# Token numbers listed as half-precision bit patterns, and both halves of the gate's weights in one product, in a graph-network, linear-attention and mixture-of-experts layer on one core

## The chip, the cores and the metric

The kernel runs on one core of one Trainium2 chip. The metric is the time of one execution on the device, in microseconds (us); lower is better. Durations of single instructions are in nanoseconds (ns) where marked so. The engines are named as the profile names them: PE (TensorE, matrix products), PEld (its weight loads), DVE (VectorE), ACT (ScalarE), POOL (GpSimd), SP (SyncE, which here only issues transfers).

## What is computed

6250 nodes with 512 features and 100000 edges, sorted by destination. With `xn` the normalised `x`:

```python
x = x + gnn(xn, src, dst) + mix(xn)           # graph part: mean over a node's in-edges, two products, norm;
                                              # mix: linear attention with 8 heads
x = x + ffn(layernorm(x))

def ffn(t):
    shared = gelu(t @ sw1.T + sb1) @ sw2.T + sb2          # 2 shared experts
    logits = t @ gate_w.T + gate_b                        # 8 routed experts
    probs = softmax(logits)
    top_v, top_i = top_k(probs, 2)
    routed = sum of top_v * expert[top_i](t)
    return shared + routed
```

The change touches two parts: `logits`, and the lists that say which tokens each of the 8 experts takes.

## The kernel before

Nodes are worked on in tiles of T = 125, two tiles (j = 0, 1) to a group, 25 groups in all (NG). Every operand of a precise product is held as a high and a low float16 half, and the helper `three` (lines 331 to 335) makes such a product of three matmuls: high by high, high by low, low by high.

The program has these stages: normalisation and keys with weight conversion (to about 396 us); **the group loop**, `group(i, prev, nxt)` on PE (line 1191), DVE (1863), ACT (872) and SP (451), beside `gathers` on POOL (line 615); a tail behind the last group, which ends the lists; the routed experts, which gather the listed tokens' rows (from line 1303 on PE, `rows_of` on POOL, line 658); and the shared experts with the sum (line 1360 on). Each engine has its own instruction stream, written out by hand; the order is fixed and semaphores alone tie the streams together.

In the group loop POOL gathers the source rows of a tile's edges with 17 indirect transfers to a tile (128 rows of 2 KB each), 9 of line 624 and 8 of line 631, 34 to a group. They go to two rings, one for j = 0 (shown as `Wff` in the profile) and one for j = 1 (shown as `region`). Before it refills a part of a ring POOL waits for PE to have used it (`agg_half`, `agg_ps`, lines 622 and 629). PE's `aggregate` (line 1135) multiplies the gathered rows with one-hot matrices (line 1151, 34 matmuls to a tile), and waits for the gathers of both parts (`gathered_a`, `gathered_b`). PE's order in `group(i, i-1, i+1)` is: the queries, the first mean turned, `aggregate(i, 1)`, the node's own product of tile 0, the second mean turned, `slot_list(prev-1, 0)`, the mean's product of tile 0, the denominators (line 1242), `turn_normalised(prev)`, the own product of tile 1, `slot_list(prev-1, 1)`, the mean's product of tile 1, `gate(prev)`, the spread denominators (line 1258), `aggregate(i+1, 0)`, `places(prev)`, the attention product.

**The gate.** PE's `gate` (line 1172) makes the logits of two tiles by `three` with 8 columns of weights `Wg`, 12 matmuls to a tile; DVE's `gate` (line 1798) scales them and adds the bias (line 1802), takes the maxima and their indices, and makes `chosen`, from which PE's `places` (line 1180) counts each token's place in its expert's list; DVE's `places` (line 1827) turns these counts into a column `posc` (which 128 places) and a row `posr` (which of them). DVE counts its steps on the semaphore `gate_dve`, 21 to a group (GATE_STEPS). In DVE's `group`, `gate(prev)` stands ahead of the scaled queries (lines 1918 and 1922), on which PE's attention product waits.

**The lists.** DVE's `listed` (line 1851) makes, for each of the two choices k of a tile's tokens, a one-hot of the column (`slot_c`, line 1859, 125 x 400 float16) and two matrices 125 x 128 that hold, at the token's row of places, the token's number within its tile (`own`, line 1860) and the first number of its tile (`tile_row`, line 1861). PE's `slot_list` (line 1123) adds four products of them into bank 7, 400 columns each (line 1127). After the last group DVE copies the bank into whole numbers (`idx_all`, line 1998), and SP (line 489) waits for that before it sends out the first list of indices (line 494), with which POOL's first gather of the routed experts begins (line 664).

In the trace `slot_p`, `slot_c`, `iota_c` and the first ring all lie in `Wff`, and `idx_all` in `ohs`.

The tail runs `gate(NG-1)`, `slot_list(NG-2, 0)`, `slot_list(NG-2, 1)`, `places(NG-1)`, the count, `slot_list(NG-1, 0)`, `slot_list(NG-1, 1)` on PE (lines 1290 to 1300), and on DVE lines 1954 to 1998.

## Time and profile before

| what | us |
|---|---|
| median of 3 runs | 2285.58 |
| lowest and highest of them | 2281.53, 2285.96 |
| the profiled execution, its time | 2284.43 |
| its span, first to last instruction | 2282.6 |
| PE busy, share of the span | 2074.4, 91% |
| DVE busy | 1567.9, 69% |
| ACT busy | 1089.6, 48% |
| POOL busy | 1323.6, 58% |

The span is what the hardware profiler recorded between the first and the last instruction; the execution's own time is 1.8 us longer, and the profiled execution lies 1.2 us under the median of the three runs. Busy time is the time in which an engine had an instruction at work; an instruction that issues a transfer to a ring on POOL counts, the wait for its data does not. The mean granted clock of TensorE was 0.972 of full speed.

### The profile page before, as it was taken

The numbers are of one execution on the slowest core, as the hardware profiler recorded it, in microseconds if no ns is written. First come the engines' busy times: TensorE is split into PE (matmuls) and PEld (weight loads), VectorE is DVE, ScalarE is ACT, GpSimd is POOL, SyncE is SP. The second block draws the span as 40 slices with busy tenths as digits, with TensorE's granted clock in tenths as the row PEclk, the third lists the DMA queues.
The fourth block names the chain that finished last, engine by engine and source line by source line (L and its number), as shares of the span: only waits on it lengthen the run. The fifth ranks groups of instructions, "written<-read, shape, count | busy, mean of one in ns | idle before, by whom it ended". The sixth has DMA issues, their size and how long they took to land. (4 is left out here: it accounts for less than half of the span.)

```text
span 2282.6 us, 46905 instructions
## 1 busy us (share of the span) xinstructions
PE 2074.4 (91%) x13232; PEld 1391.5 (61%) x13233; DVE 1567.9 (69%) x3840; ACT 1089.6 (48%) x2118; POOL 1323.6 (58%) x1370
## 2 busy tenths in 40 slices
PE   4997987899999999999999999993899999789998
PEld 2544554566666666666666666662666666557776
DVE  6887995567788777777787778775344444346666
ACT  3555674554655465546554655431344344323332
POOL 3665665777777777777777777740222222244443
PEclk9999999999999999999999999995999999989999
DMA  8647554788788788888888888873445455557675
GB/s 281 215 117 246 197 171 131 206 264 260 248 250 260 247 251 254 261 248 249 249 260 248 249 252 258 248 237 115 132 162 164 150 163 166 156 186 263 241 265 194
DMA packets 190000, 497.24 MB, mean 218 GB/s; under 512 B 42012, under 2 KB 54812, under 8 KB 188152
## 3 DMA queue, kind: packets, MB, share of 16 engines
q0 software_dynamic: 92720, 309.47, 45.6%
q1 hardware_dynamic: 66505, 135.52, 17.1%
q10 hardware_dynamic: 30719, 51.60, 6.0%
q8 instruction: 24, 0.39, 0.1%
q14 instruction: 32, 0.26, 0.0%
HBM read 373.91 MB, written 122.50 MB: 217 GB/s over the span
## 5 line engine op out<-in xcount | busy, mean ns | idle before, releaser
L664 POOL DMA_INDIRECT region<-table,idx x122 | 116.5, 955 | 359.3 <-PE bank L1315 268.9
L624 POOL DMA_INDIRECT Wff<-table,ebuf x225 | 235.7, 1047 | 69.0 <-issue 67.5
L624 POOL DMA_INDIRECT region<-table,ebuf x225 | 224.4, 998 | 84.0 <-issue 80.4
L333 PE MATMUL bank<-Wff,region 128*125 128x512 f16 (+1 forms) x636 | 245.1, 385 | 11.8 <-DVE region L2044 6.4
L631 POOL DMA_INDIRECT Wff<-table,ebuf x200 | 218.6, 1093 | 61.0 <-issue 61.0
L334 PE MATMUL bank<-Wff,region 128*125 128x512 f16 (+1 forms) x636 | 243.9, 384 | 0.0
L335 PE MATMUL bank<-Wff,region 128*125 128x512 f16 (+1 forms) x636 | 243.6, 383 | 0.0
L1151 PE MATMUL bank<-region,ohs 128*125 128x512 f16 x850 | 198.5, 389 | 45.0 <-DMA region<-table,ebuf 45.0
L631 POOL DMA_INDIRECT region<-table,ebuf x200 | 202.9, 1015 | 60.9 <-issue 60.9
L1151 PE MATMUL bank<-Wff 128*125 128x512 f16 x850 | 188.3, 380 | 0.0
L1151 PEld LDWEIGHTS bank<-region,ohs 128*125 128x125 f16 x850 | 114.5, 139 | 118.3 <-DMA region<-table,ebuf 55.6
L2009 DVE COPY region<-bank 128x1024 f16<-128x1024 f16 x60 | 41.5, 692 | 178.8 <-PE bank L1315 178.8
L333 PE MATMUL bank<-Wsn,region 128*125 128x512 f16 x400 | 152.9, 382 | 0.0
L1151 PEld LDWEIGHTS bank<-Wff 128*125 128x125 f16 x850 | 114.1, 137 | 63.5
L335 PE MATMUL bank<-Wsn,region 128*125 128x512 f16 x400 | 151.5, 379 | 0.0
L334 PE MATMUL bank<-Wsn,region 128*125 128x512 f16 x400 | 151.5, 379 | 0.0
L819 ACT ACTIVATE Wff<-iota_f,ebuf 128x125 f16<-128x125 f32 x425 | 125.9, 386 | 28.2 <-issue 28.2
L2016 DVE SCALAR_TENSOR_TENSOR region<-bank,sv,region 128x512 f32<-128x512 f32 x118 | 88.6, 750 | 71.4 <-PE bank L335 69.1
L819 ACT ACTIVATE ohs<-iota_f,ebuf 128x125 f16<-128x125 f32 x425 | 125.8, 386 | 17.9 <-DMA ebuf<-edges 14.2
L1326 PE MATMUL bank<-region,Wff 128*128 128x256 f16 x472 | 129.5, 274 | 1.9 <-DVE region L2009 1.9
L1327 PE MATMUL bank<-region,Wff 128*128 128x256 f16 x472 | 129.4, 274 | 0.0
L1328 PE MATMUL bank<-region,Wff 128*128 128x256 f16 x472 | 129.4, 274 | 0.0
(328 smaller groups left out, 5562.2 us busy)
## 6 DMA issues: line engine op xcount, KB each, us to landing
yd<-region ACTq DMA_DIRECT2D x59, 512.0 KB, 3.1
x2d<-region SPq DMA_DIRECT2D x25, 512.0 KB, 6.5
table<-region SPq DMA_DIRECT2D x25, 512.0 KB, 4.2
region<-x2d SPq DMA_DIRECT2D x25, 512.0 KB, 5.0
table<-region POOLq DMA_DIRECT2D x50, 250.0 KB, 3.4
xnt<-region POOLq DMA_DIRECT2D x25, 500.0 KB, 4.0
region<-xnt SPq DMA_DIRECT2D x25, 500.0 KB, 5.0
x2t<-region SPq DMA_DIRECT2D x25, 500.0 KB, 4.4
```

What stands on the lines that cost most here:

```text
L333: wmm(ps, xh, wh, start=first, stop=False)
L334: wmm(ps, xh, wl, start=False, stop=False)
L335: return wmm(ps, xl, wh, start=False, stop=last)
L624: pool.indirect_dma_start(out=ring[j][:, s, :], out_offset=None, in_=table, in_offset=bass.IndirectOffsetOnAxis(ap=ebuf[j][:, 2 * s:2 * s ...
L631: pool.indirect_dma_start(out=ring[j][:, s, :], out_offset=None, in_=table, in_offset=bass.IndirectOffsetOnAxis(ap=ebuf[j][:, 2 * s:2 * s ...
L664: pool.indirect_dma_start(out=tg[:, c, :], out_offset=None, in_=table2, in_offset=bass.IndirectOffsetOnAxis(ap=idx[:, 2 * turn + c:2 * tur ...
L819: act.activation(oh[j][:, s, :], iota_f[:], ACT.Abs, bias=ebuf[j][:, 2 * s + 1:2 * s + 2], scale=-1.0).then_inc(made_in, 1)
L1151: last = wmm(bank[6][0:T, :], oh[j][:, s, :], ring[j][:, s, part * D:(part + 1) * D], start=False, stop=False, skip_group_check=True)
L1326: wmm(ps, w1(e, 0, k, c), tTc[:, 0, k, :], start=(k == 0), stop=False)
L1327: wmm(ps, w1(e, 0, k, c), tTc[:, 1, k, :], start=False, stop=False)
L1328: last = wmm(ps, w1(e, 1, k, c), tTc[:, 0, k, :], start=False, stop=(k == KC - 1))
L2016: stt(ysb[:, j, :], bank[4 + j][:, :], sv[:, S_W2:S_W2 + 1], b2bc[:, e, :], ALU.mult, ALU.add).then_inc(sem["y_sb"], 1)
```

## The change

Two edits. **The lists:** a token's number plus 1024 is held as a 16-bit whole number, `id_bits`, and read as a float16 (`id_value`), so that one matrix `slot_p` for each choice takes the place of two. `slot_list` has two products in the place of four. The sum in bank 7 is copied to float16, its bits are read as whole numbers, and 1024 is taken away again (`idx_all`, now two instructions). `id_bits` is made in one DVE instruction ahead of the loop and raised by 256 in each group, and then copied to `id_value`; these take the place of `own`, of two memsets and of `tile_row`. **The gate:** the high half of a tile's rows is multiplied with both halves of the weights in one matmul of 16 columns, then its low half with the weights' high half in 8: 8 matmuls to a tile in the place of 12. The sum of the two halves' columns is made on DVE by a second `scalar_tensor_tensor`. GATE_STEPS goes from 21 to 23, and all waits on `gate_dve` go with it.

```diff
...
 I32 = mybir.dt.int32
+I16 = mybir.dt.int16
 U32 = mybir.dt.uint32
...
 HELD = 4
+ID_BASE = 1024
 OVER = NS + NE - HELD
...
         tok = sb("tok", [128, 2], I32)
-        own = sb("own", [128, 1], F32)
-        tile_row = sb("tile_row", [128, 2], F32)
+        id_bits = sb("id_bits", [128, 2], I16)
+        id_value = sb("id_value", [128, 2], F32)
         counted = sb("counted", [T, 1], F32)
...
         iota_c = over[0:T, spare:spare + COLS]
-        slot_p = over[0:T, spare + COLS:spare + COLS + 4 * 128].rearrange("p (k v n) -> p k v n", k=2, v=2)
+        slot_p = over[0:T, spare + COLS:spare + COLS + 2 * 128].rearrange("p (k n) -> p k n", k=2)
         behind = (OVER - 1) * FFB + 2 * TAIL
         slot_c = over[0:T, behind:behind + 2 * COLS].rearrange("p (k n) -> p k n", k=2)
-        assert spare + COLS + 4 * 128 <= (OVER - 1) * FFB and behind + 2 * COLS <= OVER * FFB - SLOTS // 2 * T
+        assert spare + COLS + 2 * 128 <= (OVER - 1) * FFB and behind + 2 * COLS <= OVER * FFB - SLOTS // 2 * T
         idx_all = ohs[:, 1200:1200 + 2 * COLS].bitcast(I32)
...
         den_rows = bank[2][0:TERMS, 128:128 + GT]
+        logits = bank[2][0:T, 0:4 * NE].rearrange("p (j v e) -> p j v e", j=G, v=2)
         half_ff = FFB // 2
...
             sp.wait_ge(sem["sched2_set"], 1)
-            sp.wait_ge(sem["idx_set"], 1)
+            sp.wait_ge(sem["idx_set"], 2)
             for e in range(NE):
...
             act.wait_ge(sem["yd_zero"], 16)
-            act.wait_ge(sem["disp_set"], 10)
+            act.wait_ge(sem["disp_set"], 8)
             onehots(0, 0)
...
             def gate(i):
-                act.wait_ge(sem["gate_dve"], GATE_STEPS * i + 6)
+                act.wait_ge(sem["gate_dve"], GATE_STEPS * i + 7)
                 if past(i):
-                    act.wait_ge(sem["gate_dve"], GATE_STEPS * (i - 1) + 11)
+                    act.wait_ge(sem["gate_dve"], GATE_STEPS * (i - 1) + 12)
                 for j in range(G):
...
             def slot_list(i, j):
-                pe.wait_ge(sem["slot_oh"], 12 * i + 6 * j + 6)
+                pe.wait_ge(sem["slot_oh"], 8 * i + 4 * j + 4)
                 for k in range(2):
-                    for v in range(2):
-                        last = wmm(bank[7][:, 0:COLS], slot_p[:, k, v, :], slot_c[:, k, :], start=False, stop=False, skip_group_check=True)
+                    last = wmm(bank[7][:, 0:COLS], slot_p[:, k, :], slot_c[:, k, :], start=False, stop=False, skip_group_check=True)
                 last.then_inc(sem["slot_ps"], 1)
...
                     for k in range(KC):
-                        last = three(bank[2][0:T, 8 * j:8 + 8 * j], tT[:, 0, k, both(j)], tT[:, 1, k, both(j)],
-                                     Wg[:, 0, k, :], Wg[:, 1, k, :], k == 0, k == KC - 1)
+                        wmm(logits[:, j], tT[:, 0, k, both(j)], Wg[:, :, k, :], start=(k == 0), stop=False)
+                        last = wmm(logits[:, j, 0, :], tT[:, 1, k, both(j)], Wg[:, 0, k, :], start=False, stop=(k == KC - 1))
                     last.then_inc(sem["gate_ps"], 1)
...
-                pe.wait_ge(sem["gate_dve"], GATE_STEPS * i + 9)
+                pe.wait_ge(sem["gate_dve"], GATE_STEPS * i + 10)
                 for j in range(G):
...
                 if older:
-                    pe.wait_ge(sem["gate_dve"], GATE_STEPS * (prev - 1) + 1)
+                    pe.wait_ge(sem["gate_dve"], GATE_STEPS * (prev - 1) + 2)
                 turn_mean(0)
...
                 if older:
-                    pe.wait_ge(sem["gate_dve"], GATE_STEPS * (prev - 1) + 12)
+                    pe.wait_ge(sem["gate_dve"], GATE_STEPS * (prev - 1) + 13)
                 turn_mean(1)
...
             turn_normalised(NG - 1)
-            pe.wait_ge(sem["gate_dve"], GATE_STEPS * (NG - 2) + 12)
+            pe.wait_ge(sem["gate_dve"], GATE_STEPS * (NG - 2) + 13)
             gate(NG - 1)
...
             dve.wait_ge(sem["sched_set"], 1)
-            dve.tensor_copy(own[:], tok[:, 0:1]).then_inc(sem["disp_set"], 1)
+            ts(id_bits[:], tok[:], float(ID_BASE - G * 128), None, ALU.add).then_inc(sem["disp_set"], 1)
             dve.memset(counted[:], 0.0).then_inc(sem["disp_set"], 1)
-            dve.memset(tile_row[:, 0:1], -G * 128.0).then_inc(sem["disp_set"], 1)
-            dve.memset(tile_row[:, 1:2], 128.0 - G * 128).then_inc(sem["disp_set"], 1)
             dve.wait_ge(sem["ident_set"], 10)
             dve.tensor_copy(iota_c, iota_n[0:T, :]).then_inc(sem["disp_set"], 1)
-            dve.wait_ge(sem["disp_set"], 10)
+            dve.wait_ge(sem["disp_set"], 8)
             halved(0, 0)
...
-                done, base = sem["gate_dve"], GATE_STEPS * i
+                done, base = sem["gate_dve"], GATE_STEPS * i + 1
                 dve.wait_ge(sem["gate_ps"], 2 * i + 2)
-                stt(gl[:], bank[2][0:T, 0:16].rearrange("p (j e) -> p j e", j=G), sv[0:T, S_G:S_G + 1],
+                stt(gl[:], logits[:, :, 0, :], sv[0:T, S_G:S_G + 1],
                     gateb_bc[0:T, None, :].broadcast_to([T, G, NE]), ALU.mult, ALU.add).then_inc(done, 1)
+                low_in = of(dve, base)
+                dve.wait_ge(sem["consts"], 1)
+                dve.wait_ge(done, low_in)
+                stt(gl[:], logits[:, :, 1, :], sv[0:T, S_G:S_G + 1], gl[:], ALU.mult, ALU.add).then_inc(done, 1)
                 logits_in = of(dve, base + 1)
...
-                done, base = sem["gate_dve"], GATE_STEPS * i
+                done, base = sem["gate_dve"], GATE_STEPS * i + 1
                 dve.wait_ge(sem["pos_ps"], i + 1)
...
                 stt(posr[:], posc[:], -128.0, posf[:], ALU.mult, ALU.add).then_inc(done, 1)
+                ts(id_bits[:], id_bits[:], G * 128.0, None, ALU.add).then_inc(done, 1)
+                dve.wait_ge(done, base + 21)
                 if past(i):
-                    dve.wait_ge(sem["slot_oh"], 12 * i)
-                ts(tile_row[:], tile_row[:], G * 128.0, None, ALU.add).then_inc(done, 1)
-                assert GATE_STEPS == 21
+                    dve.wait_ge(sem["slot_oh"], 8 * i)
+                dve.tensor_copy(id_value[:], id_bits[:].bitcast(F16)).then_inc(done, 1)
+                assert GATE_STEPS == 23
...
-                placed_in = of(dve, GATE_STEPS * i + 21)
+                placed_in = of(dve, GATE_STEPS * (i + 1))
                 dve.wait_ge(sem["consts"], 1)
...
                     ts(slot_c[:, k, :], iota_c, posc[:, j, k:k + 1], None, ALU.is_equal).then_inc(sem["slot_oh"], 1)
-                    ts(slot_p[:, k, 0, :], iota_c[:, 0:128], posr[:, j, k:k + 1], own[0:T, :], ALU.is_equal, ALU.mult).then_inc(sem["slot_oh"], 1)
-                    ts(slot_p[:, k, 1, :], iota_c[:, 0:128], posr[:, j, k:k + 1], tile_row[0:T, j:j + 1], ALU.is_equal, ALU.mult).then_inc(sem["slot_oh"], 1)
+                    ts(slot_p[:, k, :], iota_c[:, 0:128], posr[:, j, k:k + 1], id_value[0:T, j:j + 1], ALU.is_equal, ALU.mult).then_inc(sem["slot_oh"], 1)
...
             dve.wait_ge(sem["slot_ps"], 2 * NG)
-            dve.tensor_copy(idx_all, bank[7][:, 0:COLS]).then_inc(sem["idx_set"], 1)
+            listed_ids = gelc.rearrange("p c n -> p (c n)")[:, 0:COLS // 2].bitcast(F16)
+            dve.tensor_copy(listed_ids, bank[7][:, 0:COLS]).then_inc(sem["idx_set"], 1)
+            dve.wait_ge(sem["idx_set"], 1)
+            ts(idx_all, listed_ids.bitcast(I16), -float(ID_BASE), 0.0, ALU.add, ALU.max).then_inc(sem["idx_set"], 1)
...
-GATE_STEPS = 21
+GATE_STEPS = 23
 NORM_STEPS = 6 + 3 * NEWTON
...
```

## Rows read from the trace of the kernel before

**Rows 1.** Busy time by stretch; columns: stretch, length, engines' busy us, granted clock, DMA share.
```profile
396.00:1513.00 1117.00, 1071.19 (x6420) 725.39 (x6419) 856.15 (x2673) 616.00 (x1397) 863.41 (x833) 0.99 0.81 250
1513.00:1585.00 72.00, 42.38 (x234) 26.84 (x232) 48.63 (x191) 16.27 (x33) 4.42 (x9) 0.74 0.47 172
```

**Rows 2.** Groups of POOL, 395.6 to 1513.1 us; count, busy us, mean ns, idle before.
```profile
L624 POOL DMA_INDIRECT Wff<-table,ebuf x216 | 225.5, 1044 | 65.8 <-issue 64.3 <-DMA ebuf<-edges 1.5
L624 POOL DMA_INDIRECT region<-table,ebuf x225 | 224.4, 998 | 84.0 <-issue 80.4 <-DMA ebuf<-edges 3.4 <-PE bank L1151 0.3
L631 POOL DMA_INDIRECT Wff<-table,ebuf x192 | 211.0, 1099 | 58.5 <-issue 58.5
L631 POOL DMA_INDIRECT region<-table,ebuf x200 | 202.9, 1015 | 60.9 <-issue 60.9
```

**Rows 3.** Waits of 560 to 1570 us; us in total, times, longest.
```profile
PE bank L1151 <- DMA region<-table,ebuf: 30.7, 20, 2.5
```

**Rows 4.** Timeline of PE; start us, length us, instruction, count, idle before.
```profile
1021.12 0.84 PE L1127 MATMUL bank<-Wff 125*128 125x400 f16 x4
1021.80 0.38 PE L333 MATMUL bank<-Wsn,region 128*125 128x512 f16 x1
...
1518.38 3.67 PE L1151 MATMUL bank<-region,ohs 128*125 128x512 f16 x16 [2.47 <-DMA region<-table,ebuf]
...
1536.90 0.17 PE L333 MATMUL bank<-Wg,region 128*125 128x8 f16 x1
...
1538.20 0.20 PE L335 MATMUL bank<-Wg,region 128*125 128x8 f16 x1
...
1562.17 0.24 PE L333 MATMUL bank<-Wg,region 128*125 128x8 f16 x1 [1.25 <-ACT region L862]
...
1564.62 0.25 PE L335 MATMUL bank<-Wg,region 128*125 128x8 f16 x1
...
1568.96 1.52 PE L1127 MATMUL bank<-Wff 125*128 125x400 f16 x4 [2.74 <-DVE Wff L1861]
1570.27 0.21 PE L1185 MATMUL bank<-chosen,tri 125*125 125x8 f16 x1
```

**Rows 5.** Timeline of DVE: the instructions that the edits touch.
```profile
988.06 0.23 DVE L1802 SCALAR_TENSOR_TENSOR gl<-bank,sv,gateb_bc 125x16 f32<-125x16 f32 x1 [0.59 <-PE bank L335]
988.39 0.24 DVE L1808 MAX8 g<-gl 125x8 f32<-125x8 f32 x2
...
1567.45 0.33 DVE L1859 TENSOR_SCALAR Wff<-Wff,posc 125x400 f16<-125x400 f16 x1
...
1568.14 0.32 DVE L1859 TENSOR_SCALAR Wff<-Wff,posc 125x400 f16<-125x400 f16 x1
...
1583.47 0.56 DVE L1998 CAST ohs<-bank 128x400 int32<-128x400 f32 x1
```

**Rows 6.** Timeline of POOL in one group, gathers; the first of these is not held.
```profile
991.73 0.95 POOL L624 DMA_INDIRECT region<-table,ebuf  x1 [0.30 <-issue]
...
1013.62 1.42 POOL L624 DMA_INDIRECT Wff<-table,ebuf  x1 [0.30 <-issue]
...
1023.48 1.93 POOL L631 DMA_INDIRECT Wff<-table,ebuf  x1 [0.30 <-issue]
```

**Rows 7.** Timeline of DVE in that group: two-input instructions, and one of `listed`.
```profile
992.49 1.45 DVE L1922 TENSOR_TENSOR region<-region 128x500 f16<-128x500 f32 x2
...
1013.54 0.68 DVE L1876 TENSOR_TENSOR region<-region 128x500 f32<-128x500 f32 x1
...
1023.37 1.22 DVE L1886 TENSOR_TENSOR region<-region,beta_bc 125x1024 f32<-125x1024 f32 x1
...
1025.66 0.30 DVE L1861 TENSOR_SCALAR Wff<-Wff,posr,tile_row 125x128 f16<-125x128 f16 x1
```

**Rows 8.** Gather behind the last of these rows, on POOL.
```profile
1025.71 0.95 POOL L631 DMA_INDIRECT Wff<-table,ebuf  x1 [0.30 <-issue]
```

**Rows 9.** The stretch behind PE's wait at 466.5 us; columns as in the first group.
```profile
466.50:468.50 2.00, 2.00 (x5) 1.20 (x6) 0.00 (x0) 0.00 (x0) 1.39 (x3) 0.50 0.61 193
```

## The prediction

> **What bounds the kernel now.** I read the busy time by stretch first. The group loop, 396 to 1513 us, takes half of the time; in it PE is busy for 1071 of 1117 us at full clock, DVE for 856 and POOL for 863 [rows 1]. So PE looks like the bound, and the change takes work off PE. The rows of POOL say otherwise. Its 833 gathers take 863.8 us together, and 269 us of idle time stand before them, of which only 0.3 us was ended by PE [rows 2]. The idle time is 0.30 us before each gather [rows 6], some 250 of the 269 us, and for the rest one gap near the start of the loop: after it POOL issues gather behind gather, and never waits for a free ring. A group takes 45.7 us, 34 gathers at a pitch of 0.95 + 0.30 us (42.7 us), and 3.0 us more because some take longer than 0.95 us. PE for its part waits for gathered rows in 20 of 22 groups, 30.7 us in all [rows 3], and 2.47 us for the last gathers of all, at 1518.38 [rows 4]. **POOL's issue of gathers paces the loop**; PE has about 1.4 us to spare in each group (30.7 / 22). The tail, 1513 to 1585 us [rows 1], is a chain through DVE and PE with no such cover.
>
> **The products of the lists, on PE.** Four products of 400 columns take 1021.80 - 1021.12 = 0.68 us, 0.17 each [rows 4]. Two fewer in each of 50 tiles: 100 x 0.17 = 17 us of PE's time, 0.68 us in a group. At half clock in the tail four take 1570.27 - 1568.96 = 1.31 us [rows 4], so two fewer save 0.65.
>
> **The gate's products, on PE.** 24 small matmuls start 23 pitches apart in 1538.20 - 1536.90 = 1.30 us, 0.057 each; eight fewer save 0.46 us in a group, 11 us in 25. In the tail at half clock the pitch is (1564.62 - 1562.17) / 23 = 0.107, and eight fewer save 0.85 [rows 4]. That one product has 16 columns instead of 8 I price at nothing; if columns counted, 8 more at 2.4 GHz are 0.003 us each, 0.03 us for eight.
>
> **DVE.** One matrix fewer for each choice: two instructions of 0.23 us pitch (three starts in 1568.14 - 1567.45 = 0.69 us [rows 5]) in each tile, 0.46 us. The second instruction on the logits waits for the first; the next dependent step starts 988.39 - 988.06 = 0.33 us behind it [rows 5], so it costs 0.33. In `places` one more dependent step costs between nothing and 0.33; I take 0.2. The final list is now copied to float16 and then converted: the copy as before 0.56 us [rows 5], and behind it a step of 400 elements from SBUF that the trace does not show; between 0.3 (the 400-column step of `listed` in SBUF, 0.32 [rows 5]) and 0.65 us (a second pass like the first, with a wait), I take 0.45. Three tiny steps at the start go, next to nothing, beside POOL's gap.
>
> **In the loop** PE saves 0.68 + 0.46 = 1.14 us in each of some 24 groups, 27 us in all, and none of it reaches the end by itself: PE arrives 1.14 us earlier at rows that land when POOL has issued them, and its wait of about 1.4 us grows to 2.5, the last one from 2.47 to 3.6. What can reach POOL is one thing. A gather is held while DVE runs an instruction with two tensors from SBUF: the one of 1023.48 took 1.93 in place of 0.95 us and lies in line 1886's (1023.37 to 1024.59); the one of 1013.62 took 1.42 and lies in line 1876's (1013.54 to 1014.22) [rows 6, 7]. Both fit one rule: 0.13 us after its start a gather waits for the end of such an instruction (1024.59 - 1023.61 = 0.98; 1014.22 - 1013.75 = 0.47). Eight holds of that kind stand in the group: 0.07, 0.26, 0.20, 0.47, 0.43, 0.17, 0.98 and 0.15 us, at the lines 1922, 1930, 1935, 1876, 1796, 1707, 1886 and 1907; over the 816 gathers they make the 3.0 us a group. The change adds and removes no such instruction (the new ones read one tensor from SBUF), but it moves some. DVE is 0.81 us earlier from line 1918 to 1941 (1.14 on PE, less 0.33), 0.6 earlier at 1876 and 1796, 0.45 earlier at 1907, and not moved at 1707 and 1886, which follow PE's wait. By the rule, in the same group: line 1922 then covers the gather of 991.73 (992.36 - 991.86 = 0.50 in place of 0.07), the next ones give 0.27 and 0.19, line 1876 0.50, line 1796 misses by 0.05, 0.12, 0.98 and none: 2.56 in place of 2.73 us. That is -0.17 a group, -4 us over 24. But two of these misses are by less than 0.1 us, and each group starts from where the one before left off; I take -0.1, **-2.5 us**. Its bounds: one hold of average size (0.4) more in every group is +9.6 us, one and a half fewer -14.
>
> **In the tail** every step counts, from PE's last wait on. Two pairs of list products, -0.68, and the gate -0.46; the second logit step +0.33: -0.81 at the attention product. The last gate at half clock -0.85, its second step +0.33: -1.33. Then `listed` -0.46, its products -0.65, `places` +0.2, `listed` -0.46, products -0.65, `listed` -0.46 (each waits for the other [rows 4, 5]): -3.81. The last conversion +0.45: **-3.4 us**, bounds -2.5 and -4.5. The routed and shared experts get the same lists: nothing.
>
> **The sum.** The profiled execution took 2284.43 us, 1.2 under the median of 2285.58: 2284.43 - 3.4 - 2.5 = 2278.5 there, and 2279.7 against the median.
>
> **A rule weighed against the trace.** Line 1861's instruction at 1025.66 to 1025.96 covers the point 1025.84 of the gather of 1025.71, and that gather took 0.95 us, not held [rows 7, 8]. So I price the removal of its like at nothing for POOL. The Trainium skill (SBUF - State Buffer, the rules on the shared port pair) has a VectorE instruction in a two-port mode, which a float16 one with a single tensor can be, lock GpSimd out as well; by that the sum would have a further gain, the fifth case below. The same page has two tensors from SBUF contend with a GpSimd instruction that reads SBUF, and there the trace agrees, 0.98 us of it at line 1886.
>
> **The rivals.**
> 1. *The holds fall much lighter.* Six moved instructions cost about 1.6 us a group; if in every group one hold of the size of line 1876's stays out, it is -0.5 a group, -12: 2285.6 - 3.4 - 12 = 2270. For it: one hold (line 1796, 0.43) goes by 0.05 us already. Against: the new one at line 1922.
> 2. *The holds fall heavier: slower.* If the gathers met the moved instructions at random, each of length L would cost L x L / (2 x 1.25), 1.25 us being the pitch of the gathers; the six kinds come to 1.97 us a group against 1.6 now, +0.35, +8.4: 2285.6 - 3.4 + 8.4 = 2290.6. It decides as soon as the holds grow by more than 0.14 us a group, where they eat the tail's gain. For it: the present places are lighter than chance.
> 3. *PE's clock falls in the longer wait.* Behind a wait of PE for gathers early in the loop, the one that ends at 466.5 us, the granted clock was 0.50, half of 2.4 GHz, for at least 2 us [rows 9]. Half clock for 4 us costs PE 2 us, which its spare 2.5 us cover in the loop. Behind the last gathers nothing covers it: +2 in the tail, 2281.7. Against: over the whole loop the granted clock was 0.99 [rows 1], waits and all.
> 4. *PE paces the loop after all* and its 27 us come through: 2285.6 - 3.4 - 27 = 2255.2. Against: 0.3 us of POOL's waits are PE's [rows 2].
> 5. *The removed instructions did hold gathers.* 92 of 0.31 us in the loop, by the formula above 0.04 each, 3.5 us more: 2279.7 - 3.5 = 2276. Against: the gather of [rows 8]. The page for it is the one of the Trainium skill named above.
>
> **How the numbers follow.** What a measurement of this kernel can tell from no change is about 0.2%, 4.6 us. My forecast, with 2276 to 2284 as its own range, has 0.42, of which 0.22 lies below 2281.0 and 0.20 above. Rival 1 has 0.19, all faster; rival 2 0.16, of which 0.13 slower; rival 3 0.15, 0.12 of it the same and 0.03 faster; rivals 4 and 5 0.04 each. Faster 0.22 + 0.19 + 0.03 + 0.08 = 0.52; the same 0.20 + 0.03 + 0.12 = 0.35; slower 0.13. The range leaves out rival 4, the light end of rival 1 and the heavy end of rival 2: 2267 to 2290.
>
> **What would show it.** PE busy in the loop falls by some 27 us and its waits for gathers grow by about 1.1 us in each group; POOL still shows no idle time that PE ended; POOL's gathers have a mean near 1034 ns (now 1037); the time from the end of PE's last wait to the first copy of the list falls from 65.1 us (1583.47 - 1518.38 [rows 4, 5]) by 3.9 to 61.2, and the conversion then takes 0.45 more. Wrong would be: a POOL that waits for `aggregate`, a change in the 0.95 us of an unheld gather, or a loop that is shorter by PE's 27 us. If the mean of a gather moved by more than 10 ns, the holds decided and not the work removed.

## The result, and the profile after

The changed kernel takes 2258.42 us (median of 4 runs, 2253.56 to 2261.71), the kernel before beside it 2285.30 (4 runs, 2281.53 to 2285.96): a ratio of 0.9889, 95% interval 0.9876 to 0.9902. It is 26.9 us faster. The forecast was 5.9 us faster, and its range ended at 2267. The profiled execution took 2260.08 us.

The head of its page, then busy time by stretch (columns as in [rows 1]):

```profile
span 2258.5 us, 46325 instructions
PE 2050.2 (91%) x12932; PEld 1370.3 (61%) x12933; DVE 1552.0 (69%) x3789; ACT 1089.0 (48%) x2118; POOL 1304.6 (58%) x1370
```

```profile
396.00:1490.00 1094.00, 1045.95 (x6095) 702.92 (x6094) 834.25 (x2608) 616.99 (x1400) 840.21 (x829) 0.99 0.82 255
1490.00:1560.00 70.00, 44.61 (x266) 29.80 (x263) 51.28 (x190) 16.27 (x33) 8.71 (x13) 0.79 0.49 171
```

POOL's groups in the loop, which answer to [rows 2], and PE's waits for gathers, which answer to [rows 3]:

```profile
L627 POOL DMA_INDIRECT region<-table,ebuf x225 | 225.0, 1000 | 85.2 <-issue 84.0 <-DMA ebuf<-edges 1.2
L627 POOL DMA_INDIRECT Wff<-table,ebuf x216 | 211.0, 977 | 65.8 <-issue 62.5 <-DMA ebuf<-edges 3.3
L634 POOL DMA_INDIRECT Wff<-table,ebuf x192 | 205.2, 1069 | 58.5 <-issue 58.5
L634 POOL DMA_INDIRECT region<-table,ebuf x200 | 203.5, 1017 | 61.0 <-issue 61.0
```

```profile
PE bank L1153 <- DMA region<-table,ebuf: 28.6, 17, 2.4
```

The idle time of POOL is what it was: 0.30 us before each gather, one gap near the start, nothing that PE ended. The gathers themselves are shorter. I count from the 35th gather, the first behind that gap, to the last, 816 in all. What a gather takes over 0.95 us I call its hold, and the instant 0.125 us behind its start its point. Before, the holds add up to 70.9 us, after to 51.6 us: **19.3 us less, a mean of 1013 ns for 1037**. The gaps between them add up to 248.4 us in both. The 24.1 us by which the span fell are, from the two traces: the 35th gather 1.8 later (418.60, 420.41), holds -19.3, last gather's end to the last aggregation product +1.2, that product to the first load of the list -3.8, and the part of the experts -4.0 (697.7 to 693.7 us), which this change does not touch. In that part PE's waits for the routed experts' rows (lines 1315 and 1317) go from 44.4 to 39.8 us with the same products: 4 of the 24.1 us are no work of the edit that I can name.

A sum of the holds by the line of VectorE whose end the held gather waited for, in us over the 24 groups (some 2 us of small ones fit no line), with what the prediction's followed group would give (its holds times 24):

```
step (line before/after)    before   after   moved   forecast
beta added (1886/1891)       22.5    19.3    -3.3      0
q + rest (1876/1881)          9.8     0.6    -9.2     +0.7
low half of table (1796)      9.3     2.6    -6.7    -10.3
halves (1707/1709)            7.6     6.8    -0.8     -1.2
low half of q (1922/1927)     6.3     6.0    -0.4    +10.3
hh steps (1930,1935/1935,1940) 10.5  10.7    +0.2      0
den terms (1907/1912)         2.9     0      -2.9     -3.6
lines 1714, 1865, 1916        0.1     3.8    +3.7      0
```

One group after the change, POOL's gathers, then VectorE beside them:

```profile
1011.69 0.95 POOL L627 DMA_INDIRECT Wff<-table,ebuf  x1 [0.30 <-issue]
...
1018.07 1.43 POOL L634 DMA_INDIRECT Wff<-table,ebuf  x1 [0.30 <-issue]
...
1021.06 1.94 POOL L634 DMA_INDIRECT Wff<-table,ebuf  x1 [0.30 <-issue]
```

```profile
1011.68 0.72 DVE L1881 TENSOR_TENSOR region<-region 128x500 f32<-128x500 f32 x1 [0.40 <-ACT region L890]
...
1017.99 0.68 DVE L1709 TENSOR_TENSOR Wff<-Wff 128x1000 f16<-128x1000 f16 x1 [1.59 <-issue]
...
1020.96 1.22 DVE L1891 TENSOR_TENSOR region<-region,beta_bc 125x1024 f32<-125x1024 f32 x1
```

Two of the three gathers obey the prediction's rule: the gather of 1018.07 reaches its point at 1018.20 and waits for 1018.67, that of 1021.06 waits for 1022.18. The first does not. Its point, 1011.82, lies inside line 1881's instruction (1011.68 to 1012.40), and the gather takes 0.95 us. It is the VectorE instruction that is longer, 0.72 in place of 0.68.

The tail, PE, VectorE and SP (these answer to the last rows of [rows 4, 5]):

```profile
1502.07 1.29 PE L1153 MATMUL bank<-region,ohs 128*125 128x512 f16 x5 [1.83 <-DMA region<-table,ebuf]
```

```profile
1562.94 0.56 DVE L2004 CAST region<-bank 128x400 f16<-128x400 f32 x1
1563.54 0.37 DVE L2006 TENSOR_SCALAR ohs<-region 128x400 int32<-128x400 int16 x1
```

```profile
1564.77 0.60 SPq L497 DMA_DIRECT2D idx<-ohs  x1
```

From the end of PE's last wait to the first copy of the list it is now 60.87 us; 65.1 before, 61.2 forecast.

### The profile page after: what moved, and what is told of

Its sections match the earlier page's. It is cut to its first block and busy times, and to the rows that moved or that the text cites. A ratio compares the mean times of both kernels' runs of the same rounds, so it can differ in the third digit from the quotient of the medians.

```text
span 2258.5 us, 46325 instructions
## 1 busy us (share of the span) xinstructions
PE 2050.2 (91%) x12932; PEld 1370.3 (61%) x12933; DVE 1552.0 (69%) x3789; ACT 1089.0 (48%) x2118; POOL 1304.6 (58%) x1370
## 5 line engine op out<-in xcount | busy, mean ns | idle before, releaser
L627 POOL DMA_INDIRECT Wff<-table,ebuf x225 | 221.1, 983 | 69.1 <-issue 65.7
L634 POOL DMA_INDIRECT Wff<-table,ebuf x200 | 212.8, 1064 | 61.0 <-issue 61.0
L1153 PE MATMUL bank<-region,ohs 128*125 128x512 f16 x850 | 205.1, 398 | 41.9 <-DMA region<-table,ebuf 41.9
L338 PE MATMUL bank<-Wff,region 128*125 128x512 f16 (+1 forms) x636 | 242.9, 382 | 0.0
L338 PE MATMUL bank<-Wsn,region 128*125 128x512 f16 x400 | 151.5, 379 | 0.0
```

The lines of the kernel that those rows point to most:

```text
L338: return wmm(ps, xl, wh, start=False, stop=last)
L627: pool.indirect_dma_start(out=ring[j][:, s, :], out_offset=None, in_=table, in_offset=bass.IndirectOffsetOnAxis(ap=ebuf[j][:, 2 * s:2 * s ...
L634: pool.indirect_dma_start(out=ring[j][:, s, :], out_offset=None, in_=table, in_offset=bass.IndirectOffsetOnAxis(ap=ebuf[j][:, 2 * s:2 * s ...
L1153: last = wmm(bank[6][0:T, :], oh[j][:, s, :], ring[j][:, s, part * D:(part + 1) * D], start=False, stop=False, skip_group_check=True)
```

## Experiments

### Ten runs in which POOL did not pace the loop: e1 to h1

The theory, as the first traces gave it: POOL's gathers pace the loop, and the holds decide. Its rival: PE's shorter work was what was gained (27 us removed, 26.9 us gained, a coincidence of numbers that needed a test). Edits of the first series: the lists' part alone (e1, f2), the gate's part alone (e2), the whole change with PE's time given back (e3, f1), and the whole change with the addition of beta made on one tensor (e4, h1), which leaves beta out of the result. The two edits that are not parts of the change:

```diff
...
+                if j:
+                    for _ in range(PAD):
+                        wmm(bank[6][0:T, :], zeros16[0:1, 0:T], zeros16[0:1, :], start=False, stop=False, skip_group_check=True)
                 with pe.Fori(lo, hi) as r:
...
+PAD = 5
...
-                tt(xg, xg, beta_bc[0:T, None, :].broadcast_to([T, G, D]), ALU.add).then_inc(sem["h_gam"], 1)
+                ts(xg, xg, 1.0, None, ALU.mult).then_inc(sem["h_gam"], 1)
...
```

e1: 

> The changed kernel with the gate of before: 24 small matmuls, one DVE instruction on the logits. Theory H (holds): POOL paces the loop, so the time follows the sum of what gathers take over 0.95 us, and not PE's work; that sum can lie anywhere between 50 and 75 us, and the time is 2285 less the tail's 2 us, less the fall of that sum from 70.9 us. Theory W (work): PE's removed time comes through, 0.68 us a group, 17 us: about 2266, with the sum of holds beside the point.

e2: 

> The kernel before with the change's gate alone. Theory W: 0.46 us a group of PE's work less, 11 us: 2274. Theory H: DVE's later instructions come only 0.13 us earlier (0.46 less 0.33), so the holds stay near 70.9 us and the time near 2284; whatever it is, time and holds move by the same amount within 3 us.

e3: 

> The changed kernel with 5 matmuls of 512 columns with zeros more in each group, directly ahead of PE's wait for the second tile's gathered rows: about 1.07 us a group, 27 us of PE's work, as much as the change took away. Theory W: the whole gain is lost, 2285. Theory H: PE's wait shrinks by about 1 us a group, POOL waits for nothing, and the time stays at 2258, within the few us that moved holds make.

e4: 

> The changed kernel with the sum of x and beta replaced by a product of x with 1.0, so beta is left out of the result; DVE then reads one tensor from SBUF in place of two, in an instruction that may run in a two-port mode. It held a gather in 24 groups of 24, for 19.3 us in all. Theory H with the two-tensor rule alone: these holds go, 19 us less, about 2240. If a one-tensor instruction in a two-port mode holds as well, as the 400-column step of the lists did for 0.1 us: it is about half as long, its holds are 0.3 us on the average and some 8 us stay: 2248. Theory W: no change in the loop, 2258.

Measured, ratios to the kernel before: e1 1.0231 (1.0159 to 1.0304), e2 0.9981 (0.9941 to 1.0022), e3 1.0212 (1.0155 to 1.0270), e4 1.0039 (1.0012 to 1.0066). But **the kernel before itself took 2962.7 us** there, not 2285, and on three other chips 2963.0 (f1, f2), 3001.6 (g1 to g3) and 3004.7 (h1). The repeats gave 1.0174 (f1, as e3) and 1.0258 (f2, as e1). Then the change itself and two kernels with PE's work in the loop cut (g2 the kernel before, g3 the changed one; the products of the low halves are left out), to let POOL pace:

g1: 

> The changed kernel itself once more. In the first experiments the kernel before took 2963 us in the place of 2285, because PE waited for its own instructions inside the loop. Theory H (holds): where POOL does not pace the loop neither holds nor their fall reach the end, so the gain of the loop, 19 us, is gone, and only the tail's 4 us are left; where the kernel before takes 2285 again, the change takes 2258. Theory W (work): fewer instructions on PE are fewer to wait for, 300 of some 6700 in the loop, so the change gains more here than before, 4% of the loop's 1790 us, some 70 us.

g2: 

> The kernel before with PE's work in the group loop cut: of the queries', own, mean and attention products only high by high, and of the gathered rows only the high half is added (the result is less exact). PE has some 120 instructions and 20 us fewer in each group. Theory H: POOL paces the loop again, the gap between gathers is 0.30 us, a group takes 42.7 us and the holds, and the loop ends near 1510 us whatever PE has to do.

g3: 

> The changed kernel with the same cut. Theory H: in both thin kernels POOL paces the loop; their difference from the first gather of the loop to the last is the difference of their sums of holds within 2 us, although the change takes the same 1.14 us of PE's work a group away. Theory W: the thin changed kernel's loop is shorter by 27 us, or by nothing if PE's work is covered, with no tie to the holds.

g1 has a ratio of 0.9942 (0.9920 to 0.9964), g2 0.9066, g3 0.9024. The trace of g1 says what was different. POOL's first two groups in its loop, the loop's stretch, and PE in it:

```profile
L627 POOL DMA_INDIRECT region<-table,ebuf x225 | 227.0, 1009 | 439.3 <-DMA ebuf<-edges 361.2 <-issue 78.1
L627 POOL DMA_INDIRECT Wff<-table,ebuf x216 | 219.9, 1018 | 454.0 <-DMA ebuf<-edges 395.2 <-issue 58.8
```

```profile
396.00:2217.00 1821.00, 1312.75 (x6006) 777.25 (x6004) 825.57 (x2568) 604.14 (x1371) 823.85 (x833) 0.76 0.52 153
```

```profile
1018.04 0.27 PE L1203 MATMUL bank<-region,Wq 128*128 128x250 f16 x1
1018.67 0.27 PE L1204 MATMUL bank<-region,Wq 128*128 128x250 f16 x1 [0.36 <-issue]
1020.85 0.27 PE L1205 MATMUL bank<-region,Wq 128*128 128x250 f16 x1 [1.92 <-issue]
1023.02 0.37 PE L1203 MATMUL bank<-region,Wq 128*128 128x250 f16 x1 [1.90 <-issue]
```

Up to 1018.04 one product starts each 0.11 us; then one each 2.17 us, behind idle time that "issue" ended, so that nothing in the profile held it. Such stretches fill the loop of groups, and the granted clock falls to 0.76 with them; the last group, whose instructions are written out behind the loop, has none (its 48 query products take 5.3 us, those of a group in the loop some 22). POOL waits for edge lists, some 940 to 1030 us of gaps between the 816 gathers in place of 248. So these runs can't test which of POOL and PE paces the loop of the kernel as it ran at 2285, and none of their ratios is read. The thin kernels did not mend it: gaps of 681 and 647 us. What the runs do give is the hold itself, which needs no pace: behind the addition of beta, 10.2 to 11.4 us in e1, e2, e3 and g1, and 2.0 us in e4, where that step has one tensor. h1 was to use both:

> The changed kernel once more with the addition of beta left out (the step has one tensor in place of two, so beta is not added). In the run of the changed kernel the gathers of the group loop stood 19.3 us behind that step. Theory (POOL's gathers pace the loop, and a DVE step with two tensors holds a gather): if the kernel before takes about 2285 us again, this kernel takes 14 to 19 us less than the changed kernel's 2258, so about 2241, a ratio of 0.981 to the kernel before, and the holds behind that line fall from 19.3 to under 3 us. Rival (the holds lie in time that the loop has anyway): 2256 to 2259, ratio 0.989, though the holds fall. If the kernel before takes about 2965 us, as in the runs so far, POOL does not pace the loop, both expect a ratio of 1.00 as in e4, and the run tells the theories apart by the holds alone.

It came out at 0.9988 (0.9965 to 1.0010) beside 3004.7, holds of that line 2.9 us, within the second case of its expectation, and tells no more than e4.

### The loop written out: i1 and i2

The same instructions in the same order on every engine, without the jump back. PE's loop, one of five that are written out alike:

```diff
...
-            with pe.Fori(2, NG - 1) as i:
+            for i in range(2, NG - 1):
                 group(i, i - 1, i + 1)
...
```

i1: 

> The kernel before with the loop over the groups written out on all five engines (the same instructions in the same order, but no jump back at a group's end). In the runs so far of this series the kernel before took 2963 to 3004 us because the instructions in the body of that loop start late (48 query products 20 us, 5.0 us in the last group, which is written out). If it is the loop that makes them late, this kernel takes about 2285 us, a ratio near 0.76 to 0.78, its gathers stand back to back again (idle between the 816 about 250 us) and POOL paces the groups. If the supply is late whatever the form, it takes 2960 to 3000 us, ratio 1.00.

i2: 

> The changed kernel with the loop over the groups written out in the same way. If POOL's gathers pace it, theory (holds behind two-tensor steps of VectorE decide): 2254 to 2264 us, 24 to 30 us under the unrolled kernel before, with the time of the 816 gathers over 0.95 us near 51 us against 71 us (change of the holds equal to the change of the time before the tail within 3 us). Rival (the work removed on TensorE decides, and the holds are along for it): 24 to 30 us less though the holds differ by under 10 us. If the supply stays late: within 0.6% of the unrolled kernel before.

On this chip the kernel before took 2281.06 us with its loop as it is, so whether writing out cures the late supply stays open. Nor does the chip alone decide it: g1 to g3 and k1 to k4 below ran on the same one, with 3001.6 and 2283.0 us for the kernel before. From here on every kernel ran as the first did, at 2281 to 2284 for the one before, and POOL paced the loop. i1 took 2269.79 us, ratio 0.9957 (0.9940 to 0.9973); i2 2268.34, ratio 0.9947 (0.9930 to 0.9963). POOL's groups in the loop of i1, then of i2:

```profile
L624 POOL DMA_INDIRECT region<-table,ebuf x225 | 222.7, 990 | 83.5 <-issue 80.4 <-PE bank L1151 2.7 <-DMA ebuf<-edges 0.3
L624 POOL DMA_INDIRECT Wff<-table,ebuf x216 | 219.0, 1014 | 65.8 <-issue 65.5 <-DMA ebuf<-edges 0.3
L631 POOL DMA_INDIRECT region<-table,ebuf x200 | 206.3, 1031 | 61.0 <-issue 60.6 <-PE bank L1151 0.3
L631 POOL DMA_INDIRECT Wff<-table,ebuf x192 | 202.1, 1053 | 58.5 <-issue 58.5
```

```profile
L627 POOL DMA_INDIRECT region<-table,ebuf x225 | 221.4, 984 | 83.2 <-issue 82.6 <-DMA ebuf<-edges 0.6
L627 POOL DMA_INDIRECT Wff<-table,ebuf x216 | 218.4, 1011 | 65.8 <-issue 64.9 <-DMA ebuf<-edges 0.9
L634 POOL DMA_INDIRECT region<-table,ebuf x200 | 206.1, 1031 | 61.0 <-issue 61.0
L634 POOL DMA_INDIRECT Wff<-table,ebuf x192 | 204.7, 1066 | 58.5 <-issue 58.5
```

The busy times add up to 850.1 and 850.6 us. The holds are 57.1 us in both, and the last gather ends at 1498.38 and 1498.60. The change takes the same products off PE here and is worth 1.5 us in the medians, with the tail 4.0 shorter. I had expected i2 to keep the whole gain and the gap between the holds (51 against 71); that missed, but what theory ties together stayed together: no fall of the holds, no gain. The rival, by which the 27 us of PE count, falls. And writing the loop out is itself worth 11 us to the kernel before, with 13.8 us less of holds.

### One step with one tensor, and the gate alone: j1 and j2

j1 is i2 with e4's edit. j2 has the gate's part of the diff alone on the kernel before.

j1: 

> The changed kernel with the loop written out (2268.3 us, 816 gathers 57.1 us over 0.95 us each, 17.8 of it behind the addition of beta), with that step made on one tensor (beta is left out of the result). Nothing is taken off POOL, TensorE or the DMA. Theory (holds are the time): the holds behind that line fall to under 3 us, the sum to 41 to 46 us, and the time by as much, 11 to 16 us, to 2252 to 2257 us. Rival (VectorE's steps only happen to lie beside gathers that are long for another reason, or the time is elsewhere): 2266 to 2270 us. If the kernel before takes about 2980 us here, the run first tells whether writing the loop out cures it: then this one takes 2250 to 2270, else about 2980.

j2: 

> The kernel before with the gate's part of the change alone (both halves of the gate's weights in one product, one more step on VectorE), loop as it was. Theory (holds are the time): time before the tail changes by what the holds' sum changes from 70.9 us, whatever that is; the gate's shorter product moves VectorE's group by under 0.5 us, so I expect a sum of 58 to 72 us, and 2266 to 2283 us, the tail being shorter by about 1.6. Rival (TensorE's work is the time): 24 x 0.46 = 11 us less in the loop and 1.6 in the tail, 2270 to 2274 us, with the holds as they fall: the two are told apart by whether loop time and holds change alike to 2 us. Under a kernel before of about 2980 us: within 0.6% of it, as e2, and nothing is told.

j1: holds 57.1 to 48.0 us (-9.1), of which that line 17.8 to 6.1, more than the 3 expected (the step, now 0.68 us long, has one tensor and still held the gather at 17 of the 19 points that it covered); its gathers from the 35th to the last take 1071.6 us for 1080.7 (-9.1). The time did not move, 2268.54 us. Leaving beta out changes which experts the tokens choose, and the experts then have one step more; L338 behind the loop, i2 and then j1:

```profile
L338 PE MATMUL bank<-Wff,region 128*128 128x512 f16 (+1 forms) x436 | 168.0, 385 | 0.0
```

```profile
L338 PE MATMUL bank<-Wff,region 128*128 128x512 f16 (+1 forms) x440 | 169.0, 384 | 0.0
```

That part has 52 products more in all and takes 707.5 us in place of 697.1, which eats what the loop gains. So the total, taken by itself, speaks for the rival (2266 to 2270 expected) and against the theory (2252 to 2257), and it does so for a reason that neither had; what the holds do to the loop has to be read by the loop's own end, and there the two fall by the same 9.1 us. j2: 2280.73 us, ratio 0.9991 (0.9982 to 1.0001), holds 69.6 us (-1.3), last gather 1511.31 (-1.8). The rival had 11 us less in the loop. PE's work went and the loop stayed.

### Which part, PE's time given back, work added, a shorter step: k1 to k4

k1 and k2 are the edits of e1 and e3. The other two: k3 on the kernel before, ahead of the scaled queries (`pad` is a spare place of one number), and k4 on the changed one:

```diff
...
                     gate(prev)
+                dve.tensor_reduce(pad, gamma_bc[0:T, 0:320], AX_X, ALU.max)
...
```

```diff
...
-                tt(xg, xg, beta_bc[0:T, None, :].broadcast_to([T, G, D]), ALU.add).then_inc(sem["h_gam"], 1)
+                for j in range(G):
+                    for c in (slice(0, D // 2), slice(D // 2, D)):
+                        tt(xg[:, j, c], xg[:, j, c], beta_bc[0:T, c], ALU.add).then_inc(sem["h_gam"], 1)
...
-                dve.wait_ge(sem["h_gam"], 3 * i + 3)
+                dve.wait_ge(sem["h_gam"], 6 * i + 6)
...
```

k1: 

> The kernel before with the lists' part of the change alone (f16 bit patterns of the places, one product for each half list), loop as it was. Gate alone (j2) moved the holds by 1.3 us of 19.3, so theory expects most of the rest here: a sum of holds near 53 us and 2260 to 2266 us; if the two parts' shifts only work together, the sum stays at 65 to 71 and the time at 2276 to 2281. In either case the end of the last gather moves as the holds and the start do, to 0.5 us. Rival (TensorE's work is the time): 24 x 0.68 = 16 us less in the loop, whatever the holds do.

k2: 

> The changed kernel with five products of 512 columns of zeros added in each group on TensorE (about 1.07 us a group, what the change took off it). Theory (POOL paces, holds are the time): TensorE's time is not on the path; the holds may move with VectorE, which waits for TensorE in places, by up to 10 us either way, and the end of the last gather follows them to 0.5 us: 2252 to 2270 us. Rival (TensorE's shorter work is what was gained): 2280 to 2286 us, with the holds still near 52 us.

k3: 

> The kernel before with one reduction of 320 columns added on VectorE in each group ahead of the scaled queries (about 0.35 us; one tensor read), so that what follows lies later beside the gathers; nothing is taken away. Theory: the sum of the holds changes, by up to 20 us and in either direction, and the end of the last gather changes by the same to 0.5 us; a fall of both would show a gain from added work. Rival (VectorE's place beside the gathers is indifferent): time and last gather within 2 us of the kernel before, or later by up to 24 x 0.35 = 8 us, whatever the holds.

k4: 

> The changed kernel with the addition of beta (1.21 us, two tensors, 19.3 us of holds) in four instructions of 256 columns each. Theory (a gather waits for the end of the one instruction that runs at its sensitive point): a hold behind that line is at most 0.3 us, so 24 groups give at most 7 us and likely 4: the sum falls by 12 to 16 us, to 36 to 40, and the time to 2243 to 2248 us. If four instructions back to back hold as one does, the holds and the time stay (2258). VectorE has about 0.2 us more work a group, which ends no wait of POOL.

All runs in which POOL paced, one profiled execution each, us; "stretch" is from the 35th gather's start to the last one's end, the ratio is to the kernel before of the same chip (2281.1 beside i1 and i2, 2283.6 beside j1 and j2, 2283.0 beside k1 to k4), and the last column runs from the start of the last aggregation product to the first load of the list:

```
kernel              median us  ratio (95%)               holds  stretch  stretch-holds  last product to list
before              2285.30    1                          70.9   1094.5     1023.6        63.2
change              2258.42    0.9889 (0.9876, 0.9902)    51.6   1075.2     1023.6        59.4
i1 before, unrolled 2269.79    0.9957 (0.9940, 0.9973)    57.1   1080.7     1023.6        63.9
i2 change, unrolled 2268.34    0.9947 (0.9930, 0.9963)    57.1   1080.7     1023.6        59.9
j1 i2, no beta      2268.54    0.9930 (0.9913, 0.9946)    48.0   1071.6     1023.6        59.9
j2 gate alone       2280.73    0.9991 (0.9982, 1.0001)    69.6   1093.2     1023.6        62.6
k1 lists alone      2257.70    0.9895 (0.9879, 0.9912)    48.6   1072.1     1023.5        59.9
k2 change, PE pad   2260.72    0.9897 (0.9880, 0.9915)    60.0   1083.6     1023.5        60.2
k3 before + work    2275.49    0.9966 (0.9954, 0.9979)    65.6   1089.1     1023.5        63.1
k4 beta in quarters 2251.68    0.9864 (0.9848, 0.9881)    37.9   1061.5     1023.6        60.2
```

The stretch less its holds is 816 times 0.95 us and 248.4 us of gaps. That it is the same to 0.2 us in ten kernels means that POOL never waited for PE or for edges behind the gap near the start, with 27 us more or less of PE's work; the whole difference of the loops is the holds.

k1: the lists' part alone has the whole gain, 2257.7 us, more than expected (holds 48.6 for "near 53"). k2: with 1.07 us given back to PE in each group it stays at 2260.7, where the rival had 2280 to 2286. Its four runs lie between 2255.7 and 2268.4, and the profiled one is the slowest, with 60.0 us of holds: PE's pace moves VectorE's steps, so the holds, either way. k3: **work added, and 7.5 us faster** in the medians, the holds 5.3 us less and the stretch 5.4. Its profiled execution too is the slowest of its runs, 2281.07 us, 3.4 under the one profiled of the kernel before; the holds of an execution near the median are not on record for k2 and k3. k4: the holds behind beta fall from 19.3 to 2.1 us, the sum to 37.9 as expected, the stretch by 13.7; the time, 2251.68, is 6.7 us under the change and misses the expected 2243 to 2248, because the part of the experts took 700.2 us against 693.7. That part lies between 692.6 and 700.2 us in the nine kernels with the same lists. The difference is mostly PE's wait for the routed experts' gathered rows: 39.1 to 41.0 us in the five kernels at or below 695.3 us, 41.9 to 46.3 in the other four, and 46.3 in k4 for 39.8 in the change. Why the rows come later isn't shown. k4 is the fastest kernel here and leaves nothing of the computation out. Its POOL groups at line 634 and PE's waits of 560 to 1550 us for ACT's mean and for gathers, then one quartered step and the gather beside it:

```profile
L634 POOL DMA_INDIRECT region<-table,ebuf x200 | 209.7, 1048 | 61.0 <-issue 61.0
...
L634 POOL DMA_INDIRECT Wff<-table,ebuf x192 | 187.7, 978 | 58.5 <-issue 58.5
```

```profile
PE bank L1212 <- ACT region L832: 23.9, 21, 1.4
...
PE bank L1153 <- DMA region<-table,ebuf: 0.3, 1, 0.3
```

```profile
1011.54 1.42 DVE L1893 TENSOR_TENSOR region<-region,beta_bc 125x256 f32<-125x256 f32 x4
```

```profile
1011.64 1.14 POOL L634 DMA_INDIRECT Wff<-table,ebuf  x1 [0.30 <-issue]
```

The gather is let go after 0.19 us, though VectorE's four pieces run back to back for 1.42: it waits for the one piece that runs, not for a pause. PE's wait for gathers, 28.6 us in the change, comes to one of 0.3 us in the same stretch, and PE waits for ACT's mean (line 832) in its place, so a further fall of the holds may meet the work of PE and ACT; no run tried it.

## Why the prediction was wrong

**Right: what paces the loop.** POOL's issue, its 0.30 us gaps, and PE's 1.14 us a group worth nothing by themselves (i1 and i2, j2, k2). Rival 4 gave 2255.2, near the result, and is the one that the runs exclude most plainly. The prediction's own sign, "if the mean of a gather moved by more than 10 ns, the holds decided", came out at 24 ns.

**Right: the tail.** Forecast -3.4, measured -3.8 from the last aggregation product to the list's load; the gate's part alone -0.6, the lists' alone -3.3. Kernels with the same tail differ by up to 0.8 there. Rival 3's fall of the clock cost nothing that shows: the mean granted clock over the loop stayed at 0.99, and over the tail it was 0.79 (1490 to 1560 us) for 0.74 (1513 to 1585 us). The conversion's second step takes 0.37 us, inside its bounds.

**Wrong: the term "-0.1 a group, -2.5 us".** It measured -19.3 us, -0.80 a group, below even its bound of -14. The term rests on one followed group, moved by the forecast shifts (-0.17 a group), and on a rule of when a gather is held. Three steps of it failed.
1. *"line 1876 0.50".* The shift that I had worked out put this instruction 0.18 us ahead of the gather's point, and the rule made that a hold of 0.50. It came to lie 0.12 to 0.16 us ahead in 20 of 24 groups, and there is no hold: 9.2 us. The rule lacks its front edge. Before the change the trace showed it already, POOL and then VectorE:

```profile
561.71 0.95 POOL L624 DMA_INDIRECT Wff<-table,ebuf  x1 [0.30 <-issue]
```

```profile
561.74 0.68 DVE L1876 TENSOR_TENSOR region<-region 128x500 f32<-128x500 f32 x1 [0.40 <-ACT region L887]
```

   The point, 561.84, is covered, and the gather takes 0.95 us. I counted the covered points whose holds fitted, and not those that had none. One of line 1796's two instructions lies at this edge too after the change (0.147 us ahead of the point, and 0.744 us long in place of 0.68), where I had it missed by 0.05.
2. *"line 1922 0.50 in place of 0.07".* That was one group's place. The next point lies anywhere from 0.01 to 1.24 us behind the start of this step's two instructions, from group to group, and the sum hardly moved (6.3 and 6.0 us). A followed group says something of a step that sits at one offset in nearly all groups (line 1886: 0.22 to 0.24 us in 22 of 24), and little of a step that does not.
3. *"not moved at 1707 and 1886".* Line 1891, which was 1886, lost 3.3 us: the gather's point lies 0.29 us behind its start in the median group, for 0.23 before, and up to 0.90 in some.

Since the sum of a few signed holds was small, an error in one of them was the size of the whole. Rival 1 had the mechanism and the cause, "one hold of the size of line 1876's stays out", at -12 us and a chance of 0.19; the sum of the rest made it 19. Which side of the edge a step falls on hangs on 0.04 us, and in the written-out loops the same edit moved the holds by nothing. So one trace could hardly give the size, but the range could have been put wider: the ten kernels of the table have holds of 38 to 71 us. A mean by chance meetings, as rival 2 had, was a start; with the lengths in the trace (0.68, 0.75, 0.75, 0.68 and 0.69 us twice each, 0.42 once) its formula gives 2.08 us a group and not 1.97, which changes nothing here.

**Wrong: PE's waits for gathers "grow by about 1.1 us in each group".** They went from 30.7 to 28.6 us. The loop itself shrank by 0.80 us a group; PE's busy time fell by 0.93 (862.1 to 859.0 us between 560 and 1450 us, at groups of 45.6 and 44.8 us), for 1.14 forecast; and part of the slack now stands before the product that waits for ACT's mean, 6.3 us in seven groups for 1.5 in two.

**Rival 5** was half right. The removed instructions, 128 columns with two scalars by pointer, cover 44 points in the trace before and 44 in j2 and hold none. But the 400-column step of the same helper, float16, one tensor and one pointer, held the gather at all 72 points that lay 0.16 us and more behind its start in the change, i2, j1 and k4 together, by about 0.1 us each; before the change it happened to cover none, and in i1 one such point passed free, beside an instruction of 0.37 in place of 0.32 us. For that step the trace agrees with the Trainium skill (SBUF — State Buffer, the rules on the shared port pair), which has a two-port VectorE operation hold GpSimd off; the rule counts such one-tensor steps in general and sets no form like the first apart, and there the runs show no hold. The same section of the Trainium skill says that whichever of the two starts first has the pair for its whole instruction. As to the order the trace agrees, and that is the front edge that I left out. As to the length it agrees only where VectorE is first: where the gather is first, VectorE is 0.04 to 0.07 us late and not the gather's 0.95 us.

## What to carry to other kernels

Where POOL issues gathers back to back, sum what they take over their shortest time and sort it by the VectorE instruction that ended it; in this kernel that sum, not the work taken off the busiest engine, is what an edit elsewhere moved, and it moved by luck of place. Cut a long two-tensor step into pieces before tuning anything for its place: in k4 four pieces took 17 of the 19 us off that step's holds, 13.7 off the loop and 6.7 off the time. And before crediting a gain to an edit, give back its work (k2) and shift its neighbours (i1, k3): a gain that is gone when the loop is written out, as here, belongs to the kernel's present timing.

## What the runs showed of the hardware

**The hold has an order.** Counted over the ten kernels of the table, for the steps of 0.68 us with two tensors from SBUF: of 100 that started 0.10 to 0.145 us before a gather's point (its start + 0.125 us) none held it, and they took longer, from 0.685 us at 0.10 up to 0.74 at 0.145. Between 0.145 and 0.17, 26 of 97 held. From 0.17 on the gather waited for the end of the instruction, to 0.025 us, in 655 of 656 cases in which that end lay over 0.04 us behind the point. Under 0.10 us neither was slowed, but for two gathers of 87 that took 0.02 and 0.05 us more.

**By the counts, where the second tensor lies decides.** In the same ten kernels, at points 0.18 us or more behind an instruction's start and over 0.04 us ahead of its end: steps with two tensors from SBUF held the gather at 1519 of 1519 points, steps with one from SBUF and one from PSUM (lines 1893, 1918 and 1941 of the kernel before, the most of them) at none of 747.

**Instructions in a long loop can arrive late**, one each 2.17 us on PE, for whole stretches of every group, in the runs e1 to h1, where the kernel before took some 700 us longer; in the others, with the same kernel before, and once on the same chip, they did not. The cause isn't shown.
